# Softmax attention with sixteen 8-wide heads: scores in two passes, keys on the partitions, values on column strips

## The reference

```python
def _L3_attn_ref(x, ln_g, ln_b, Wq, bq, Wk, bk, Wv, bv):
    H = 16
    B, T, D = x.shape                      # 8, 256, 128
    xn = (x - mu) * rsqrt(var + EPS) * ln_g + ln_b
    q = (xn @ Wq + bq).reshape(B, T, H, D // H)      # k and v alike
    attn = jnp.einsum('bnhd,bmhd->bnmh', q, k) / sqrt(D // H)
    w = jax.nn.softmax(attn, axis=2)
    y = jnp.einsum('bnmh,bmhd->bnhd', w, v).reshape(B, T, D)
    ...
x = x + _L3_attn_ref(_layernorm(x), ...)
```

## Time and profile before

| | |
|---|---|
| median of three runs | 2652.94 us (2652.61 to 2653.31) |
| profiled execution | 2657.79 us |
| its span, first to last instruction | 2656.0 us |
| PE busy in the span | 2196.2 us, 83% |
| DVE, ACT, POOL busy | 1520.8, 1019.4, 131.7 us |
| the attention stage | from 2261 us to 2556.7 us in the span |

### The profile page before, as it was taken

One profiled execution on the slowest core, in us unless ns is written; L12 is line 12 of the kernel. 1 busy time (PEld: TensorE's weight loads), 2 busy tenths in 40 slices (PEclk: granted clock), 3 DMA queues, 4 the chain that ended last, 5 costly groups with the idle time before them and its releaser, 6 DMA issues. The chain is left out here.

```text
span 2656.0 us, 41675 instructions
## 1 busy us (share of the span) xinstructions
PE 2196.2 (83%) x14500; PEld 1781.7 (67%) x14500; DVE 1520.8 (57%) x3849; ACT 1019.4 (38%) x2391; POOL 131.7 (5%) x191
## 2 busy tenths in 40 slices
PE   3588777766996787499899989999989986698885
PEld 2344444436996323499899958888789983588873
DVE  6633344375666899766632227777632228577757
ACT  2244333333222332122344435555534435344434
POOL 2100000020000100100000000000000000000000
PEclk9777666677997999599899989999989989799978
DMA  5000000000000000000000014434300000000000
GB/s 155 1 1 0 0 1 0 0 28 1 1 0 1 0 0 0 32 1 0 1 1 0 0 48 126 129 118 127 104 1 0 0 1 0 1 1 0 0 1 16
DMA packets 47123, 59.70 MB, mean 22 GB/s; under 512 B 7089, under 2 KB 44690, under 8 KB 46324
## 3 DMA queue, kind: packets, MB, share of 16 engines
q1 hardware_dynamic: 47023, 58.43, 7.3%
HBM read 32.20 MB, written 26.21 MB: 22 GB/s over the span
## 5 line engine op out<-in xcount | busy, mean ns | idle before, releaser
L1680 ACT ACTIVATE a_p<-psum,a_nmax 128x256 f32<-128x256 f32 x256 | 100.4, 476 | 143.2 <-DVE a_nmax L1737 143.2
L1630 PE MATMUL psum<-a_va,a_pT 128*128 128x121 f32 x1024 | 135.7, 288 | 10.9 <-DVE a_pT L1741 6.4
L701 ACT ACTIVATE m2a_hid<-psum,m_b 128x256 f32<-128x256 f32 x256 | 100.5, 475 | 114.4 <-PE psum L55 114.3
L701 ACT ACTIVATE m2b_hid<-psum,m_b 128x256 f32<-128x256 f32 x256 | 100.5, 475 | 114.3 <-PE psum L55 114.3
L1630 PEld LDWEIGHTS psum<-a_va,a_pT 128*128 128x128 f32 x1024 | 125.5, 200 | 17.7 <-DVE a_pT L1741 7.1
L686 PE MATMUL psum<-m_w,m2a_hid 128*128 128x128 f32 x1024 | 126.2, 277 | 0.0
L686 PE MATMUL psum<-m_w,m2b_hid 128*128 128x128 f32 x1024 | 126.2, 277 | 0.0
L719 DVE SCALAR_TENSOR_TENSOR m2b_acc<-psum,m2b_gates,m2b_acc 128x128 f32<-128x128 f32 x128 | 39.0, 347 | 148.7 <-PE psum L686 148.7
L719 DVE SCALAR_TENSOR_TENSOR m2a_acc<-psum,m2a_gates,m2a_acc 128x128 f32<-128x128 f32 x128 | 39.0, 347 | 148.3 <-PE psum L686 148.3
L686 PEld LDWEIGHTS psum<-m_w,m2a_hid 128*128 128x128 f32 x1024 | 122.1, 194 | 0.6
L686 PEld LDWEIGHTS psum<-m_w,m2b_hid 128*128 128x128 f32 x1024 | 122.1, 194 | 0.6
(11 more groups left out here) (600 smaller groups left out, 5835.3 us busy)
## 6 DMA issues: line engine op xcount, KB each, us to landing
a_scratch<-a_pos SPq DMA_DIRECT2D x64, 384.0 KB, 2.7
a_shifted<-a_scratch SPq DMA_DIRECT2D x64, 256.0 KB, 3.1
m_w<-in_m_w SPq DMA_DIRECT2D x1, 2048.0 KB
arena<-in_m_w SPq DMA_DIRECT2D x1, 2048.0 KB, 8.8
arena<-in_m_up SPq DMA_DIRECT2D x1, 1760.0 KB, 7.0
a_w<-in_a_w SPq DMA_DIRECT2D x1, 1536.0 KB, 7.7
out<-X SPq DMA_DIRECT2D x1, 1024.0 KB, 5.1
m_down<-in_m_down SPq DMA_DIRECT2D x1, 880.0 KB
```

Source lines behind the costliest of these rows:

```text
L701: last = nc.scalar.activation(hid[:, e % 2, c * SEQ:(c + 1) * SEQ], ps_up(e % 2)[:, c * SEQ:(c + 1) * SEQ], ACT.Gelu, bias=m.m2_b1[:, e * ...
L1630: last = nc.tensor.matmul(ps_av(t, 2 * g + k), pT[:, g % 4, 2 * k + kt, t * P:(t + 1) * P], va[:, u, kt, h * VW:h * VW + STREAM], start=(k ...
L1680: last = nc.scalar.activation(p[:, g % 2, k, :], ps_s(g)[:, k, :], ACT.Exp, bias=nmax[:, g % 2, k:k + 1])
```

## The change

Scores are computed twice. A first pass (`plain_scores`, `ps_plain`, one head in a PSUM bank, two banks in turn) gives queries by keys, from which DVE takes only the negated maxima (`maxima`, 128 x 2 x 256). They are written as a high and a low part into two of the free slots of the query stack (`shift`); the key stack has ones there, so the second product is already score minus maximum. The query stack is turned again (`turn_shifted`) and moved by ACT, and `scores` multiplies with the keys as weights, so that keys lie on the partitions. The exponential is then one instruction of 1024 columns without a bias, and its result needs no transpose. `values` takes the values of four heads as weights of 32 columns, each on its own strip of the array, with the exponentials as moving columns; ACT moves the strips (`move_values`), PE turns them back (`turn_back`), DVE divides (`normalise`). `turn`, `evacuate` and `end` go. Of a unit's preparation, the plain pass of unit n+1 lies in g = 4 to 7 of unit n, four heads a group, and `turn_stack` in g = 3, with three PSUM banks.

What is cut from the diff is the other buffers and semaphores and the bodies that are taken out, which stand above in the kernel.

```diff
-    HEADS, HD, GROUPS = 16, 8, 8
-    VW = HD + 1
-    STREAM = SEQ - (HEADS - 1) * VW
-    VPAD = (HEADS - 1) * VW + STREAM
+    HEADS, HD, GROUPS, STRIP = 16, 8, 8, 32
...
+        st = sbr("st", [P, PAIR, 2, HEADS, 4 * HD])
+        kT, q_plain, q_shifted = sbr("kT", [P, 2, 4, SEQ]), sbr("q_plain", [P, 4, SEQ]), sbr("q_shifted", [P, 4, SEQ])
+        va = sb("va", [P, 2, PAIR, HEADS, STRIP])
+        nmax = sb("nmax", [P, HEADS, PAIR])
...
+        ps_plain = lambda h: m.psum[:, 4 + h % 2, :].rearrange("p (t f) -> p t f", t=PAIR)
+        ps_av, ps_back = m.psum[:, 6, 0:SEQ], m.psum[:, 6, SEQ:2 * SEQ]
+        ps_v = m.psum[:, 5, 0:SEQ]
...
+                pe.wait_ge(st_ready, n + 1)
+                for r in range(4):
+                    if r == 3:
+                        pe.wait_ge(moved, 4 * n + 1)
+                    turn_heads(ps_stack(r), 1 - r // 2, r % 2).then_inc(turned, 1)
+                pe.wait_ge(moved, 4 * n + 2)
+                for t in range(PAIR):
+                    last = nc.tensor.matmul(ps_v[:, t * P:(t + 1) * P], xT[:, t * P:(t + 1) * P], m.a3_v[:, :], start=True, stop=True)
                 last.then_inc(v_ready, 1)
+            def plain_scores(u, n, h):
+                if h == 0:
+                    pe.wait_ge(moved, 4 * n + 4)
+                elif h == 1:
+                    pe.wait_ge(va_ready, n + 1)
+                else:
+                    pe.wait_ge(nmax_ready, HEADS * n + h - 1)
+                rows, j = slice(STRIP * (h % 4), STRIP * (h % 4 + 1)), h // 4
+                for t in range(PAIR):
+                    last = nc.tensor.matmul(ps_plain(h)[:, t, :], q_plain[rows, j, t * P:(t + 1) * P], kT[rows, u, j, :], start=True, stop=True)
+                last.then_inc(plain_ready, 1)
+            def turn_shifted(u, n, half):
+                pe.wait_ge(shift_ready, 2 * n + half + 1)
+                turn_heads(ps_x, 0, half).then_inc(shift_turned, 1)
...
+                if g in (0, 4):
+                    pe.wait_ge(shift_moved, 2 * n + g // 4 + 1)
+                if g > 1:
+                    pe.wait_ge(e_ready, GROUPS * n + g - 1)
+                elif not isinstance(n, int) or n:
+                    pe.wait_ge(e_ready, GROUPS * n + g - 1)
+                for t in range(PAIR):
+                    for k, (rg, j) in enumerate(heads_of(g)):
+                        rows = slice(STRIP * rg, STRIP * (rg + 1))
+                        last = nc.tensor.matmul(ps_s(g)[:, 2 * k + t, :], kT[rows, u, j, t * P:(t + 1) * P], q_shifted[rows, j, :], start=True, stop=True)
                 last.then_inc(s_ready, 1)
-            def turn(n, g, prev):
...
+            def values(u, n, j):
+                pe.wait_ge(e_ready, GROUPS * n + 2 * j + 2)
+                if j or not isinstance(n, int) or n:
+                    pe.wait_ge(o_ready, 4 * n + j)
+                for t in range(PAIR):
+                    for rg in range(4):
+                        last = nc.tensor.matmul(ps_av[STRIP * rg:STRIP * (rg + 1), :], va[:, u, t, 4 * rg + j, :],
+                                                pT[:, (2 * j + rg // 2) % 4, 2 * (rg % 2) + t, :], start=(t == 0), stop=(t == 1))
+                last.then_inc(av_ready, 1)
+            def turn_back(u, n, j):
+                pe.wait_ge(av_moved, 4 * n + j + 1)
+                for t in range(PAIR):
+                    last = nc.tensor.transpose(ps_back[:, t * P:(t + 1) * P], ov[:, j % 2, t * P:(t + 1) * P], m.ident[:, :])
+                last.then_inc(back_ready, 1)
...
             def unit(u, n, prev, next):
                 for g in range(GROUPS):
+                    if g == 1:
+                        turn_shifted(u, n, 1)
                     if g < GROUPS - 1:
                         scores(u, n, g + 1)
-                    if next and g == 6:
-                        turn_stack(1 - u, n + 1, 2)
-                    if g > 1:
-                        values(u, n, g - 2)
-                    elif prev:
-                        values(1 - u, n - 1, GROUPS + g - 2)
-                    turn(n, g, prev)
-                    if next and g in (1, 2):
-                        {1: start_a, 2: start_b}[g](1 - u, n + 1)
-                    if next and g in (4, 5, 6):
-                        turn_stack(1 - u, n + 1, {4: 0, 5: 1, 6: 3}[g])
-                    if next and g == GROUPS - 1:
-                        start_c(1 - u, n + 1)
+                    if g == 0 and prev:
+                        values(1 - u, n - 1, 3)
+                    if g == 1 and prev:
+                        turn_back(1 - u, n - 1, 3)
+                    if g == 1 and next:
+                        start_a(1 - u, n + 1)
+                    if g == 2 and next:
+                        start_b(1 - u, n + 1)
+                    if g in (2, 4, 6):
+                        values(u, n, g // 2 - 1)
+                    if g == 7 and next:
+                        turn_shifted(1 - u, n + 1, 0)
+                    if g in (3, 5, 7):
+                        turn_back(u, n, g // 2 - 1)
+                    if g == 3 and next:
+                        turn_stack(1 - u, n + 1)
+                    if g > 3 and next:
+                        for h in range(4 * g - 16, 4 * g - 12):
+                            plain_scores(1 - u, n + 1, h)
+                    if g == 7 and next:
                         scores(1 - u, n + 1, 0)
...
+            def move_stack(u, n):
+                for r in range(4):
+                    act.wait_ge(turned, 4 * n + r + 1)
+                    to = q_plain[:, :, :] if r > 1 else kT[:, u, :, :]
+                    nc.scalar.activation(to[:, 2 * (r % 2):2 * (r % 2) + 2, :], ps_stack(r), ACT.Copy).then_inc(moved, 1)
+            def move_shifted(u, n, half):
+                act.wait_ge(shift_turned, 2 * n + half + 1)
+                nc.scalar.activation(q_shifted[:, 2 * half:2 * half + 2, :], ps_x, ACT.Copy).then_inc(shift_moved, 1)
             def exps(n, g):
-                act.wait_ge(nmax_ready, GROUPS * n + g + 1)
-                for k in range(4):
-                    last = nc.scalar.activation(p[:, g % 2, k, :], ps_s(g)[:, k, :], ACT.Exp, bias=nmax[:, g % 2, k:k + 1])
-                last.then_inc(e_ready, 1)
-            def move_stack(u, n, r):
-                act.wait_ge(turned, 4 * n + r + 1)
-                nc.scalar.activation(stT[:, u, r // 2, 2 * (r % 2):2 * (r % 2) + 2, :], ps_x, ACT.Copy).then_inc(moved, 1)
+                act.wait_ge(s_ready, GROUPS * n + g + 1)
+                nc.scalar.activation(pT[:, g % 4, :, :], ps_s(g), ACT.Exp).then_inc(e_ready, 1)
+            def move_values(u, n, j):
+                act.wait_ge(av_ready, 4 * n + j + 1)
+                nc.scalar.activation(ov[:, j % 2, :], ps_av, ACT.Copy).then_inc(av_moved, 1)
...
             def unit(u, n, prev, next):
                 for g in range(GROUPS):
-                    if g < GROUPS - 1:
-                        exps(n, g + 1)
-                    elif next:
-                        exps(n + 1, 0)
-                    if next and g == 1:
+                    if g == 1:
+                        move_shifted(u, n, 1)
+                    exps(n, g)
+                    if g == 0 and prev:
+                        move_values(1 - u, n - 1, 3)
+                    if g in (2, 4, 6):
+                        move_values(u, n, g // 2 - 1)
+                    if g == 1 and next:
                         start_b(1 - u, n + 1)
-                    if next and g in (4, 5, 6):
-                        for r in {4: (0,), 5: (1,), 6: (2, 3)}[g]:
-                            move_stack(1 - u, n + 1, r)
...
                 nc.vector.tensor_tensor(qk[:, :, :], ps_x, m.a3_bqk[:, :].unsqueeze(1).to_broadcast([P, PAIR, 2 * D]), ALU.add)
+                nc.vector.memset(st[:, :, 0, :, 3 * HD:3 * HD + 2].bitcast(F32), 0.0)
...
-            def maxima(n, g):
-            def evacuate(n, g):
-            def end(u, n):
...
+            def maxima(u, n, h):
+                dve.wait_ge(plain_ready, HEADS * n + h + 1)
+                nc.vector.tensor_reduce(nmax[:, h, :], ps_plain(h), AX.X, ALU.max, negate=True).then_inc(nmax_ready, 1)
+            def shift(u, n, half):
+                nc.vector.drain()
+                heads = slice(8 * half, 8 * half + 8)
+                low = nmax[:, heads, :].rearrange("p h t -> p t h")
+                nc.vector.tensor_copy(st[:, :, 0, heads, 3 * HD], low)
+                nc.vector.drain()
+                nc.vector.tensor_tensor(st[:, :, 0, heads, 3 * HD + 1], low, st[:, :, 0, heads, 3 * HD].bitcast(F32), ALU.subtract).then_inc(shift_ready, 1)
+            def normalise(u, n, j):
+                dve.wait_ge(back_ready, 4 * n + j + 1)
+                back = ps_back.rearrange("p (t k f) -> p t k f", t=PAIR, f=STRIP)
+                nc.vector.reciprocal(rec[:, :, :], back[:, :, :, HD])
+                nc.vector.drain()
```

(77 more changed lines are left out.)

87 lines of the change are left out of this document (23 added, 64 removed).

## The result

The changed kernel takes 2640.82 us, the median of five runs (2635.29 to 2642.39), against 2652.94 on the same chip: a ratio of 0.9942 with a 95% interval of 0.9931 to 0.9953. It is 12 us faster, inside the range, but the forecast was 2616, so a third of the expected gain came. The profiled execution took 2637.31 us.

The account below looks back on a forecast made before the run. PE bounds the stage now by instruction count; after the change the chain between engines decides. From 2289.8 us, seven units of 30.0 plus 20 end the stage at 2519.8 instead of 2556.7, 37 less: 2616 us, range 2594 to 2648.

Parts of the forecast that it names:

- The costs on DVE and ACT: Per-instruction prices in the changed stage: 0.686 us per 512-element DVE reduction, 1.01 us per 1024-column ACT exponential.
- A plain pair: Two score matmuls of one head on PE in the plain pass, priced at 0.38 us at 2.4 GHz, 0.58 at 1.2.
- The pitch: Time per head in the plain pass: about 0.61 us at 2.4 GHz, as fast as DVE, and 0.70 at 1.2.
- The walk at 2.4 GHz: Chain between engines through one unit: first reduction at 13.7 us, plain pass 13.4, unit 27.2 us.
- Start and end: Stage outside the seven-unit loop: unit 0's reductions end at 2289.8 us, last unit takes 20, stage ends at 2519.8.
- Which clock: Share of stage time at 1.2 GHz, argued from PE's gaps: a third, giving 29.3 us a unit, 30.0 with lags.
- the prediction's own formula: Unit time from clock shares: 1 / (0.67/27.2 + 0.33/34.7) = 29.3 us, using unit times at 2.4 and 1.2 GHz.
- Rival 2: Stage mostly at 1.2 GHz: 33 to 34.7 us a unit, 22 at the end, 2638 to 2651; chance 0.21.
- the grouped stage: Existing attention stage with 32-row strips, used as clock evidence: clock 0.74, falling to 0.50 after PE idles 1.95 us.
- Rival 1: Gaps don't lower the stage's clock: 27.2 to 28.3 us a unit, 2594 to 2603; chance 0.20.
- Rival 3: Plain pass as relay without PE/DVE overlap: 1.21 us a head, 2693, deciding from about 0.9; chance 0.09 with other waits.
- A switch between strips and the whole array: Tiling-mode changes on PE, charged nothing; if about eight each cost 0.16 us, unit 1.3 longer and result 2626.

Follow-up runs that it names:

- e5: Changed kernel with the plain pass contracting over all 128 rows instead of the head's 32, so maxima are of four heads' summed scores; ratio to before 0.9814.
- e3: Changed kernel with unread filler matmuls on PE both after plain pairs of the next unit and before turn_stack; ratio to before 1.0164.
- e10: Changed kernel with plain-pass queries in a block layout, zero outside a head's 32 rows, so pairs use 128 rows with the full result; ratio to before 0.9926.
- e11: Changed kernel with zero-padded block layout, DVE's end_b and normalise reordered, and two plain pairs per group ahead of scores and values; ratio to before 0.9782.
- e13: Changed kernel with all 128 rows in the plain pass, DVE's end_b and normalise reordered, and plain pairs first on PE; ratio to before 0.9771.
- e1: Changed kernel with two unread 256-column matmuls on PE after each plain pair of the next unit, 24 a unit; ratio to before 1.0145.
- the two orders alone: Changed kernel with end_b behind start_c, normalise(1) and (2) ahead of maxima, and two plain pairs per group ahead of scores and values; ratio to before 0.9827.

## Why the prediction was right and where it was wrong

- **The costs on DVE and ACT** were right to a few hundredths of a microsecond. So was `values` (1.07 and 1.93). A plain pair was not: 0.50 us at 2.4 GHz, not 0.38, since the row it was taken from the earlier trace rows has two matmuls side by side on different strips. The pitch is 0.64 and 0.79 a head instead of 0.61 and 0.70.
- **The walk at 2.4 GHz** was right: 27.2 us a unit, against 27.7 in e5 at a clock of 1.00, and in both halves (13.9 to the first reduction where 13.7 was forecast, 13.5 for the pass where it was 13.4).
- **Start and end** were right: the sixteenth reduction of unit 0 ends at 2290.2 (2289.8 was forecast), and the last unit takes 21.1 us (20), from 2518.05 to 2539.15.
- **"Which clock" is the step that failed**, the share of time at 1.2 GHz and so the unit: (2518.05 - 2290.17) / 7 = 32.55 us instead of 30.0, or 17.9 of the 19.3 us by which the stage ends late (2539.15 instead of 2519.8). A clock of 0.64 is 72% of the time at 1.2 GHz, not 33%; in the prediction's own formula 1 / (0.28/27.2 + 0.72/34.7) = 32.2. Rival 2 names the time that came (2638 to 2651), though its unit begins at 33.
- **The reason behind that step was wrong too.** It argued from gaps of PE: a third, less than in the grouped stage, since PE has more to do. Gaps filled with matmuls left the clock at 0.63. The plain pass on all rows, its waits left nearly as they were, brought it to 0.94, and fewer rows pulled it down in the kernel before, where PE is busy for nine tenths of the time. The grouped stage at 0.74 has 32-row scores as well; whether these are its cause, or its gap of 1.95 us, wasn't run.
- **Rival 1** would have been right for e5. The Trainium skill's rule on idle gaps (TensorE: Matmul & The Clock Gate, "Why this matters for your kernels") lets the clock fall only behind idle gaps longer than those of this stage. The traces disagree: 0.64 in after, where PE's longest wait in the loop is 2.23 us, and 0.63 in e3, where it is 0.9. The measurement decides.
- **Rival 3** is out: two reductions in 1.29 us and a wait of 0.28 are 0.79 a head at 1.2 GHz, below the 0.9 from which it decides, and 0.64 at 2.4.
- **A switch between strips and the whole array** was charged with nothing, on a wrong reading: the four of L1606 in 0.43 us are not 4 x 256 columns one after another. Two of them run side by side, as the records of the first two show, which together last 0.38:

```profile
2298.51 0.38 PE L1606 MATMUL psum<-a_stT 32*128 32x256 f32 x2
```

So the columns are two times 256, 0.21 us at 2.4 GHz, half of the 0.43 is something else, and the row doesn't exclude a switch. In after, the plain pair enters 1.00 us after `values` began (2434.44 to 2435.44), where the walk had 0.88. A tenth of a microsecond at such a place is visible; whether a drain at the switch is its cause isn't shown. That the walk matches e5 to 0.5 us a unit bounds all of these together, unless other errors hide them.

- The span is 20.8 us shorter (2656.0 to 2635.2), the stage's end 17.5 us earlier (2556.65 to 2539.15). The other 3.3 us are in the stage behind it, whose code is the same; up to its first power of POOL it takes 31.4 us at a clock of 0.78, where it took 34.2 at 0.66. Why it begins at a higher clock is open.

Not settled: what the chip counts. The runs show what all rows do against a quarter or a half of them, not a law. The order of the work moves the clock as well, up from e10 to e11 and perhaps down from e5 to e13. Matmuls on all rows beside the 32-row ones (e1, e3) didn't help, and why is open.

## What to carry to other kernels

Don't read a PE cost at 2.4 GHz off a kernel of full-array matmuls and carry it to one of 32-row matmuls: price both levels, and look at the granted clock of a stage of the same kernel that already has such shapes. Where a contraction is short and the clock is down, try it on all rows, padded with zeros. It has a price: two heads no longer run side by side (0.74 us for 0.50), and the moves that build the layout come on top, so that the padding alone gave 0.993, hardly less than the 0.994 without it, and the gain came only together with the new orders. Gains from two causes don't add up: from 0.994, the two orders alone came to 0.983, all rows alone to 0.981, both to 0.977 (the last two intervals overlap).

## What was not expected of the hardware

- The granted clock depended on the rows that matmuls use, at the same count, columns and order of instructions: 0.64 with 32 rows in the plain pass, 0.66 with 64, 0.94 with 128; over six units of the kernel before, 0.96 with 128 rows in the value products and 0.64 with 32, between 0.50 and 0.81 by units.
- Keeping PE busy for 95% of the time did not raise it: 0.63 with fillers, 0.64 without.
- Rows that hold zeros did as rows that hold 0.5: clock 0.73 and 0.75.
- Matmuls of 32 rows on different strips ran side by side, those of two heads in the time of one: 0.50 us for four as for two, at 2.4 GHz.
